# Two scatter banks lent to path sums for 28 paths of block 1, with block 0's scatters moved behind them

## The reference

```
x1 = layernorm(x)[src]      # 4352 edges x (16 segments of 32)
x2 = edge_attr_512          # 4352 edges x (16 segments of 32)
for p in 64 paths (i1, i2, i3):
    edge_out[:, i3] += coeff[p] * x1[:, i1] * x2[:, i2]
x = x + segment_sum(edge_out, dst, 256 nodes)
```

## Time and profile before

| | us |
|---|---|
| median of 3 runs | 276.3 |
| profiled execution | 276.32 |
| its span | 274.5 |
| TensorE busy | 263.9 (96%) |
| VectorE busy | 223.8 (82%) |
| ScalarE busy | 168.5 (61%) |

### The profile page before, as it was taken

One profiled execution on the slowest core, in us unless ns is written; L12 is line 12 of the kernel. 1 busy time (PEld: TensorE's weight loads), 2 busy tenths in 40 slices (PEclk: granted clock), 3 DMA queues, 4 the chain that ended last, 5 costly groups with the idle time before them and its releaser, 6 DMA issues.

```text
span 274.5 us, 5669 instructions
## 1 busy us (share of the span) xinstructions
PE 263.9 (96%) x1639; PEld 185.3 (67%) x1639; DVE 223.8 (82%) x662; ACT 168.5 (61%) x341; POOL 39.6 (14%) x52
## 2 busy tenths in 40 slices
PE   6999999999999899998999999989999989999996
PEld 4566798886444799996778786756665654468633
DVE  5977665299657999999999999999999987655272
ACT  6931341010526999978878787499999719343260
POOL 4000150060006766661000000000000000000000
PEclk9999999999999999999999999999999999999999
DMA  6699990000014755555342000014444439000002
GB/s 205 213 412 405 445 420 25 0 2 1 1 38 127 204 171 153 156 157 152 92 142 76 2 1 1 2 36 141 162 152 152 148 87 352 21 2 2 2 0 76
DMA packets 12592, 33.91 MB, mean 124 GB/s; under 512 B 3345, under 2 KB 3602, under 8 KB 12306
## 3 DMA queue, kind: packets, MB, share of 16 engines
q1 hardware_dynamic: 10482, 26.73, 27.1%
q0 software_dynamic: 2080, 6.82, 8.9%
HBM read 32.50 MB, written 1.05 MB: 122 GB/s over the span
## 4 chain that ended last, share of the span: by engine, by line
PE 83%; DVE 9%; issue 3%; ACT 2%; DVEq 1%; DMA 1%; ACTq 0%; SPq 0%
PE psum L1348 15%; PE psum L1295 14%; PE psum L1249 10%; PE psum L1351 8%; PE psum L1273 5%; DVE big L1040 4%; PE psum L1278 4%; PE psum L1301 3%; PE psum L1422 3%; PE psum L1448 3%; PE psum L1192 3%; PE psum L1178 2%; PE psum L1132 2%; PE psum L1339 2%; PE psum L1230 1%
## 5 line engine op out<-in xcount | busy, mean ns | idle before, releaser
L1295 PE MATMUL psum<-big,dst_oh 128*128 128x512 f32 x108 | 50.7, 594 | 0.5 <-DVE big L1040 0.5
L606 ACT ACTIVATE prod<-edges,coef_b 128x320 f32 (+1 forms) x78 | 43.8, 594 | 10.6 <-PE psum L1351 9.1
L1348 PE MATMUL psum<-prod,ident 128*128 128x128 f32 x160 | 32.1, 295 | 1.0 <-DVE prod L1030 0.9
L1348 PEld LDWEIGHTS psum<-prod,ident 128*128 128x128 f32 x160 | 24.5, 190 | 10.2 <-issue 9.4
L1030 DVE TENSOR_TENSOR prod<-big,prod 128x320 f32<-128x320 f32 (+1 forms) x53 | 29.4, 556 | 0.5 <-issue 0.3
L1295 PEld LDWEIGHTS psum<-big,dst_oh 128*128 128x128 f32 x108 | 18.7, 191 | 15.1 <-issue 14.3
L1249 PE MATMUL psum<-edges,big 128*128 128x256 f32 x128 | 28.3, 381 | 0.0
L1040 DVE TENSOR_TENSOR big<-big,prod 128x64 f32 (+2 forms) x80 | 26.8, 335 | 0.0
L606 ACT ACTIVATE xparts<-edges,coef_b 128x320 f32 (+1 forms) x48 | 26.1, 589 | 1.0 <-PE psum L1348 0.8
L1249 PEld LDWEIGHTS psum<-edges,big 128*128 128x128 f32 x128 | 24.1, 190 | 3.5 <-issue 0.3
L471 POOL DMA_INDIRECT big<-xn_rows,big x16 | 17.0, 1061 | 30.5 <-DMA xn_rows<-xn 23.5
(11 more groups left out here) (223 smaller groups left out, 529.4 us busy)
## 6 DMA issues: line engine op xcount, KB each, us to landing
big<-in_w SPq DMA_DIRECT2D x3, 2048.0 KB, 16.6
edges<-in_edge SPq DMA_DIRECT2D x1, 3584.0 KB, 23.9
edges<-in_f SPq DMA_DIRECT2D x7, 512.0 KB, 3.4
edges<-in_edge SPq DMA_DIRECT2D x1, 2560.0 KB, 23.7
edges<-in_edge SPq DMA_DIRECT2D x5, 512.0 KB, 3.5
edges<-in_f SPq DMA_DIRECT2D x1, 2560.0 KB, 9.8
big<-in_f SPq DMA_DIRECT2D x4, 512.0 KB, 3.6
big<-in_gnn_w SPq DMA_DIRECT2D x1, 1024.0 KB, 6.1
```

What stands on the lines that cost most here:

```text
L606: nc.scalar.activation(slot(n)[:, 0:BLOCKS[b], :], segment(edges_of(b), single_column(words, p)), ACT.Copy, scale=coef_b[:, p:p + 1]).then ...
L1295: last = mm(bank[2 + h], dst_oh[:, n % DR, h * P:(h + 1) * P], tile_sums(b, t), start=False, stop=False)
L1348: last = mm(path_sums(to), ident[:], product[:, 0:PT].rearrange("p t u -> p (t u)"), start=False, stop=True, skip_group_check=True)
```

## The change

- In paths 0 to 27 of block 1 (MID = 28), TensorE also adds tiles 6 and 7 (MID_TILES = 2), with a third identity matmul of 64 columns into banks 2 and 3 (mid_sums). VectorE adds six tiles there and not eight.
- Both banks are cleared by TensorE ahead of path 0, once all eight banks of block 0 are copied.
- Ahead of path 39's coefficient product, ScalarE waits for 28 summed paths and copies banks 2 and 3 into the first two tiles of rest_sums (copy_mid, semaphore mid_out). From path 28 on VectorE adds eight tiles again, on top of these; it waits for mid_out first. VectorE's clearing of rest_sums covers two tiles and not four.
- VectorE multiplies paths 29 to 32 ahead of addition 28 (MID_AHEAD = 4), then adds 28 to 31 without a product between.
- The scatters of block 0 run behind paths 29, 32, 35, 38, 41, 45, 48, 51, 54 and 57. The first waits for mid_out. ScalarE's one_hot copies move with them: in the new order those for scatters 12, 13 and 14 come ahead of paths 1, 4 and 7 of block 2, where the old order had that for 14 ahead of path 5.
- The fillers behind odd paths end with path 27.

```diff
+    MID, MID_TILES, MID_AHEAD = 28, 2, 4
...
+        def mid_sums(k):
+            return product_sums(psum[:, 2 * 512:4 * 512], MID_TILES * U, k)
...
-            return [-1] * EARLY[b] + [1 + i * (NP - 4) // n for i in range(n)]
+            lo = MID + 1 if b == 1 else 1
+            return [-1] * EARLY[b] + [lo + i * (NP - 3 - lo) // n for i in range(n)]
...
+            def copy_mid():
+
+                act.wait_ge(psums, NP + MID)
+                for i in range(2):
+                    nc.scalar.activation(
+                        rest_sums[1][:, 0:MID_TILES, i * D // 2:(i + 1) * D // 2].rearrange("p t (k u) -> p k t u", u=U),
+                        bank[2 + i].rearrange("p (k t u) -> p k t u", t=MID_TILES, u=U), ACT.Copy).then_inc(mid_out, 1)
...
+                if b == 1 and p == MID + SLOTS - 1:
+                    copy_mid()
...
-            nc.vector.memset(rest_sums[1][:, 0:4, :], 0.0).then_inc(cleared[1], 1)
+            nc.vector.memset(rest_sums[1][:, MID_TILES:4, :], 0.0).then_inc(cleared[1], 1)
...
-                v = segment(rest_sums[b], out_column(words[b], p))
-                nc.vector.tensor_tensor(v, v, slot(n)[:, KEPT[b]:BLOCKS[b], :], ALU.add).then_inc(sums, 1)
+                if n == NP + MID:
+                    dve.wait_ge(mid_out, 2)
+                lo = MID_TILES if b == 1 and p < MID else 0
+                v = segment(rest_sums[b][:, lo:, :], out_column(words[b], p))
+                nc.vector.tensor_tensor(v, v, slot(n)[:, KEPT[b] + lo:BLOCKS[b], :], ALU.add).then_inc(sums, 1)
...
+            multiplied = 0
             for n in range(NP * NB):
-                if n + 1 < NP * NB:
-                    multiply(n + 1)
+                ahead = max(n + 1, NP + MID + MID_AHEAD if n >= NP + MID else 0)
+                while multiplied < min(ahead, NP * NB - 1):
+                    multiplied += 1
+                    multiply(multiplied)
                 add(n)
...
                 if n == 0:
-
+                    pe.wait_ge(mid_out, 2)
                     for h in range(H):
                         mm(bank[2 + h], ident[:], xs[:, h, :], start=True, stop=False)
...
+                for q in (2, 3) if b == 1 else ():
+                    pe.wait_ge(block_out, banks_before(1))
+                    mm(bank[q], zero_b[:], dst_ohb[:, 0:2, :].rearrange("p t n -> p (t n)"), start=True, stop=True)
...
+                    if b == 1 and p < MID:
+                        last = mm(mid_sums(to), ident[:],
+                                  product[:, KEPT[b]:KEPT[b] + MID_TILES].rearrange("p t u -> p (t u)"),
+                                  start=False, stop=True, skip_group_check=True)
                     last.then_inc(psums, 1)
-                    if KEPT[b] > PT and b and p % 2 and p < NP - 1:
+                    if b == 1 and p < MID and p % 2:
                         mm(bank[4][:, 0:N], zero_b[:], iota_b, start=False, stop=True, skip_group_check=True)
```

More of the change, by code:

```diff
@@ L356, in graph_and_experts @@
         block_out = sem("block_out")
+        mid_out = sem("mid_out")
         scattered, x3_ready = sem("scattered"), sem("x3_ready")
```

## The result

The changed kernel takes 283.28 us (median of 283.21 to 283.66) against 276.3: the ratio is 1.0254, 95% interval 1.0242 to 1.0266, slower by 7.0 us. Forecast were 282.8 us and a range of 280.9 to 284.6.

What follows compares the result with a forecast made beforehand. VectorE was taken to set the pace in block 1, but TensorE's later scatters to hold up ScalarE's clearing and block 2: 276.3 + 6.5 = 282.8 us, range 280.9 to 284.6.

Steps and rivals of the forecast that it cites:

- The scatter chain: TensorE, block 1 from 151.66: xs, ten scatters and 28 paths take 31.3 us, releasing ScalarE's clearing at 183.2, +6.4 us.
- The third pair: TensorE, block 1 paths 0 to 27: the added 64-column pair costs 0.22 us, a path 0.69 with half a filler.
- rival (b): Third pair nearly free on TensorE; path 27 waits for its product, 1.5 us earlier: 281.3 us, chance 0.12.
- The seam: Start of block 2: products wait behind ScalarE's late clearing; VectorE idles some 6 us, starts path 64 at 187.0, 5.8 late.
- VectorE's side: Block 1: shorter additions save 1.85 us, additions in a row lose 0.87, the mid_out wait 0.5; gain 0.5, swallowed by idling.
- Rival (c): TensorE's clock halves after idling near block 2's start, 2.6 us more per stretch: 284 to 286 us; 0.09 together with (d).
- Rival (a): TensorE's new work is hidden and VectorE decides, if the tenth scatter is done by about 177.3: 275.8 or 274.5; chance 0.04.
- The end: After block 2's start both sides run 6.4 to 6.7 us late, taken as 6.5; nothing behind gives it back.

Runs made afterwards that it cites:

- e1: Changed kernel with block 0's tiles 4 to 9 scattered first and the clearing waiting for six scatters: 281.97 us, 1.0101 of the kernel before in its group.
- e3: Kernel before with only the changed kernel's scatter positions and fillers, no third matmul or bank copies: 286.17 us, 1.0249 of the kernel before in its group.
- e4: Changed kernel with one of two matmuls left out of each block 0 scatter: 280.05 us, 1.0034 of the kernel before in its group.

## Why the prediction was right

**The scatter chain.** Right to 0.1 us: the clearing was forecast at 183.2 and started at 183.26 net. Its terms hold too: path 0 at 131.03 (130.68 plus the shift), copies at 150.74 (150.37 plus the shift), first scatter work at 151.95 (151.66 plus 0.29). The identity pass of xs took 1.79 us from start to start (153.74 less 151.95), against 1.72. TensorE's wait ahead of it was 0.38 us and not 0.7, as its path 29 was done at 151.2 net and not at 150.9; the copies decide the start, so this cost nothing.

**The third pair.** Right: 28 paths with 14 fillers take 150.57 less 131.03, 19.54 us, 0.698 each, where 0.22 a pair gave 0.69. By the Trainium skill (TensorE: Matmul & The Clock Gate, Back-to-back issue gap), with about 60 cycles for a matmul of up to 64 columns, the pair would have been much cheaper, as in rival (b). The trace does not agree: it has 0.22. The forecast gives this rival's time once as 281.4 and once as 281.3, from the same step; nothing hangs on it.

**The seam.** Right in mechanism, shown by e1 and e3. VectorE's path 0 of block 2 was forecast at 187.0, it is 187.2 net; path 6 6.7 late, it is 6.8 (192.73 less 185.59 and 0.36).

**VectorE's side.** The gain of 0.5 us was too large: path 33's product starts at 154.06 net against 127.15 + 31 x 0.873 = 154.2, a gain of 0.15, and path 63's at 180.33 (180.69 less 0.36) against 180.38, a gain of 0.05. The row of before is:

```profile
180.38 0.64 DVE L1030 TENSOR_TENSOR xparts<-big,xparts 128x448 f32<-128x448 f32 x1
```

The terms that were mis-sized are the additions in a row, 0.66 apart and not 0.62, and the wait, 0.57 in the profile but 0.66 from where the addition could have started. 1.85 less 0.66 less three times 0.33 is 0.2. It had no part in the result, since 5.9 us of idle time follow.

**The clock.** Rival (c) happened in the profiled execution and cost nothing that can be measured, where it was priced at 1.2 us or more. The clock fell, the scatter took 1.25 us longer and path 0 of block 2 came at 193.69, 1.2 after the forecast 192.1 and its shift. But ScalarE's coefficient products of paths 6 and on did not wait for it (ScalarE has no idle time from 183.62 to 204), and executions at either mean clock are equal. That TensorE's idle time brings the fall, as rival (c) has it, isn't shown: e3 has the same idle time and no fall, e4 the fall without such an idle time.

**Rival (a)'s bound.** By its own terms (180.9 less 0.15, 0.55 and 3.13) the tenth scatter would have to be done by 177.1 and not 177.3. The sum has 183.2, so it changes nothing.

**The end.** I took 6.5 between 6.4 and 6.7 on the ground that TensorE, less late, would give some back; VectorE's last addition is 6.9 late net. Of the 0.4 missing, 0.2 are that choice, and path 6 was 6.8 late and not 6.7; what made the last 0.1 in block 2 was not tried.

## What to carry to other kernels

Work that is moved later on one engine moves the release of every buffer that it reads; look up who reuses these buffers and what stands behind that wait in its queue, before counting what the freed time brings. A wait that is covered, as 3.13 us here, has a slack that can be read off: when its result is ready against when it is taken (0.6 us here, none six paths on). If the release has to be late, free first what is reused first: reordering the scatters alone won back 3.9 of 7.0 us.

## What the runs showed of the hardware

- Two dependent additions on VectorE without other work between them start 0.65 to 0.66 us apart at 256 columns (0.43 of work, 0.23 idle); with an independent product between them an addition costs 0.33. Products in a row, which wait for nothing of VectorE's own, start 0.53 apart.
- A float32 identity matmul of 64 columns, with its weight loads, takes TensorE as long as one of 128: 0.22 us from weight load to weight load, and 28 of them more made a path of 0.47 us one of 0.70.
- The granted clock averaged 0.64 between 188 and 192 us, behind 2.24 us in which TensorE did nothing; a scatter then took 3.13 us instead of 1.88. In e3, behind 2.23 us of the same, it stayed at 1.00 (1.98 us), and in e4 it was 0.51 from 184 to 186 us behind gaps of at most 0.35 us (3.21 us). The length of the last gap alone doesn't tell whether the clock falls.
- The kernel before took 276.3 us in one group of runs and 278.8 in two others. The eight traces of these two have the loss at one place in block 0, 2.5 to 2.8 us by the copies of block 0's last banks; its cause is open.
